# An attention and feed-forward kernel: attention's rows go through HBM, the stream is normalised on ScalarE, idle products stand in the fill, and every engine's order is new

## What is computed

```python
def reference(x, ln_w, ln_b, w_q, w_kv, w_o, theta, weight, bias):
    x = x + layernorm(attention(layernorm(x), ...))
    x = x + layernorm(ffn(layernorm(x), weight, bias))
    return x

# attention: 16 heads of 16, h = layernorm(x) * ln_w + ln_b
q, k, v = rope(h @ w_q), rope(h @ w_k), h @ w_v
s = k @ q.T * 16**-0.5                # per head
t = 1 + s + 0.5 * s * s               # a second-order "softmax"
wv = (t / t.sum(-1)) @ v
out = wv @ w_o
# ffn: rows and weights are rounded to a 6-bit grid in blocks of 32, then multiplied
out = dequantised(x) @ dequantised(weight).T + bias
```

## Time and profile before

| | |
|---|---|
| median of three runs | 645.11 us (644.78 to 649.38) |
| the profiled execution | 651.11 us |
| its span, first to last instruction | 648.8 us |
| mean granted TensorE clock | 0.985 |
| busy: PE, DVE, ACT, POOL | 615.9, 594.8, 530.0, 449.3 us |

### The profile page before, as it was taken

How to read it: one execution, slowest core, us unless ns; L and a number is a source line. 1 busy time by engine, 2 the same in 40 slices (tenths; PEclk the granted TensorE clock), 3 DMA queues, 4 the chain that set the end, 5 groups by cost and what they waited for, 6 DMA issues and landing times. The chain is left out here.

```text
span 648.8 us, 20724 instructions
## 1 busy us (share of the span) xinstructions
PE 615.9 (95%) x6620; PEld 457.7 (71%) x6620; DVE 594.8 (92%) x1489; ACT 530.0 (82%) x1448; POOL 449.3 (69%) x785
## 2 busy tenths in 40 slices
PE   6889999999999999999999999999999999999974
PEld 5666667676776776777777777767777766788763
DVE  5799899899899989999999999989999999987796
ACT  4347788888788897989888888978888888999973
POOL 3475466677777878788777867767877777765464
PEclk9699999999999999999999999999999999999996
DMA  7101031222223232232323232223223212230201
GB/s 245 34 2 42 20 76 30 72 63 65 50 72 88 70 91 68 75 84 67 62 67 83 77 86 73 69 57 101 60 68 92 76 39 41 68 91 18 68 26 49
DMA packets 52362, 43.51 MB, mean 67 GB/s; under 512 B 7201, under 2 KB 48545, under 8 KB 52257
## 3 DMA queue, kind: packets, MB, share of 16 engines
q1 hardware_dynamic: 51440, 41.42, 24.1%
q10 hardware_dynamic: 816, 0.79, 0.4%
HBM read 18.65 MB, written 8.39 MB: 42 GB/s over the span
## 5 line engine op out<-in xcount | busy, mean ns | idle before, releaser
L1168 ACT ACTIVATE feat<-ps_f 128x512 f32<-128x512 f32 x256 | 144.4, 599 | 4.9 <-PE ps_f L852 4.3
L691 DVE TENSOR_TENSOR kf<-kf 128x896 f32<-128x896 f32 (+1 forms) x128 | 131.2, 1027 | 1.8
L852 PE MATMUL ps_f<-qT,selr 128*128 128x512 f32 x320 | 122.1, 435 | 1.8 <-ACT qT L1236 1.3
L691 POOL TENSOR_TENSOR kf<-kf 128x224 f32<-128x224 f32 x64 | 76.5, 1195 | 13.3 <-DVE kf L1515 11.1
L1015 PEld LDWEIGHTS ps_mt<-kf,vp 128*32 128x32 f32 x2048 | 64.1, 110 | 30.0 <-issue 28.3
L1015 PE MATMUL ps_mt<-kf,vp 128*32 128x153 f32 x2048 | 79.7, 296 | 0.6 <-DVE kf L691 0.6
L1725 POOL TENSOR_TENSOR qsp<-kf,qsp 128x256 fp32r<-128x256 f32 x64 | 58.6, 916 | 9.8 <-ACT qsp L1259 9.6
L852 PEld LDWEIGHTS ps_f<-qT,selr 128*128 128x128 f32 x320 | 52.8, 190 | 15.2 <-issue 11.0
L913 PE MATMUL ps_o<-feat,main 120*32 120x512 f32 x448 | 59.7, 604 | 0.0
L916 PE MATMUL ps_o<-feat,rm 128*32 128x512 f32 x448 | 58.6, 593 | 0.0
L788 PE MATMUL ps_qk<-wkqv_h,hT_l 128*128 128x512 f32 x128 | 52.4, 409 | 3.3 <-DVE wkqv_l L1425 3.3
(11 more groups left out here) (199 smaller groups left out, 1885.2 us busy)
## 6 DMA issues: line engine op xcount, KB each, us to landing
xc<-L_attn_x SPq DMA_DIRECT2D x16, 512.0 KB, 4.5
result<-fin SPq DMA_DIRECT2D x64, 128.0 KB, 2.0
xa<-L_attn_x SPq DMA_DIRECT2D x15, 512.0 KB, 4.1
heads_out<-osb SPq DMA_DIRECT2D x224, 32.0 KB, 2.0
shares<-sums SPq DMA_DIRECT2D x112, 64.0 KB
sums<-osb SPq DMA_DIRECT2D x224, 2.0 KB
wkqv<-L_attn_w_kv ACTq DMA_DIRECT2D x2, 256.0 KB, 4.9
xa<-L_attn_x SPq DMA_DIRECT2D x1, 384.0 KB, 6.2
```

The costliest lines, as they stand in the source:

```text
L691: return eng.tensor_tensor(dims(row, F_MAIN, [[FW, heads], [HD, NR - 1], [1, HD]]), dims(row, F_LIN, [[FW, heads], [0, NR - 1], [1, HD]]), ...
L852: pe.matmul(ps_f[i % 2][:, :], selr[:, i], queries, start=True, stop=True).then_inc(sel_done, 1)
L1168: act.activation(feat[:, p2, i], ps_f[i % 2][:, :], ACT.Square).then_inc(squared, 1)
```

## The change

1. `move_quad` issues one transfer per quad, all of a quad's osb, 256 KB, into a tensor in HBM (`rows`). New on SP, once per sequence: `fetch_heads` brings the denominators into `sums` (one transfer) and the results into `heads_out` (two of 256 KB, with a head's dimension outermost, so that a partition is dimension times heads plus head); `store_inverses` writes the reciprocals to HBM; `spread_shares` reads them back as two transfers of 256 KB for all four tiles. `normalise_attention` waits for both. `copy_quad` waits until osb's last content has been moved. The rows of w_o are loaded in the same new order, and the path of the last two sequences writes in it.
2. `normalise_x` moves from DVE to ACT, as Identity with a scale and a bias per partition. The bias, minus mean times rstd, is a new instruction on POOL, `shift_x`. `rstd_x` and `shift_x` wait until z of two tiles before is made.
3. `IDLE["fill"]` has 15 entries at PE's places 1 to 32: 30 products of 128 columns.
4. `constant` and `rest_terms` are split in two each (`sum_linear`, `scale_terms`); `weight_size` waits for `turn_ready`.
5. All places in `ORDER` are new. A sequence takes 58 places on PE, 75 on ACT, 81 on DVE, 52 on POOL and 13 on SP.

```diff
 ORDER = {
...
+IDLE = {"fill": (1, 1, 1, 4, 4, 6, 7, 10, 14, 19, 23, 24, 32, 32, 32,), "drain": ()}
...
-            sp.dma_start(wo[:], w_o.rearrange("(c p) n -> p c n", p=P)).then_inc(wo_in, 16)
+            for c in range(CH):
+                sp.dma_start(wo[:, c], w_o.rearrange("(h d) n -> d h n", d=HD)[:, c * HC:(c + 1) * HC]).then_inc(wo_in, 16)
...
             def move_quad(t):
-                par, quad, s = t.par, t.tile, t.seq
-                if quad == 0:
-                    wait(sp, norm_ready, NT * (s - 1))
-                    for tile in range(NT):
-                        wait(sp, shares_in[tile], 16 * CH * s)
+                par, quad = t.par, t.tile
+                wait(sp, heads_in[par], 16 * CH * (t.load - 1))
+                wait(sp, sums_in, 16 * (t.seq - 1))
                 sp.wait_ge(o_copied, t.n)
-                for part in range(NT):
-                    sp.dma_start(sums[part * H + HQ * quad:part * H + HQ * (quad + 1)],
-                                 osb[HD:P:VW, par, quad, part * P:(part + 1) * P]).then_inc(sums_in, 16)
-                for h in range(HQ):
-                    row = HD * (HQ * (quad % 2) + h)
-                    sp.dma_start(heads_out[row:row + HD, par, quad // 2], osb[VW * h:VW * h + HD, par, quad]).then_inc(heads_in[par], 16)
+                sp.dma_start(rows[par, quad], osb[:, par, quad]).then_inc(moved[par], 16)
+
+            def fetch_heads(t):
+                par, s = t.par, t.seq
+                wait(sp, inverses_out, 16 * s)
+                sp.wait_ge(moved[par], 16 * NQ * t.load)
+                by_row = rows[par].rearrange("q (h r) n -> r (q h) n", r=VW)
+                sp.dma_start(sums[:, :], by_row[HD]).then_inc(sums_in, 16)
+                wait(sp, norm_ready, NT * (s - 1))
+                for c in range(CH):
+                    sp.dma_start(heads_out[:, par, c], by_row[0:HD, c * HC:(c + 1) * HC]).then_inc(heads_in[par], 16)
+
+            def store_inverses(t):
+                s = t.seq
+                for c in range(CH):
+                    wait(sp, shares_in[c], 16 * s)
+                sp.wait_ge(inverted, s + 1)
+                sp.dma_start(inverses, sums[:, :]).then_inc(inverses_out, 16)
 
             def spread_shares(t):
                 s = t.seq
+                sp.wait_ge(inverses_out, 16 * (s + 1))
                 wait(sp, norm_ready, NT * s)
-                sp.wait_ge(inverted, s + 1)
-                for tile in range(NT):
-                    for c in range(CH):
-                        first = tile * H + c * HC
-                        sp.dma_start(shares[:, c, tile * P:(tile + 1) * P],
-                                     dims(sums[first:first + HC, 0:1], 0, [[0, HD], [1, P]])).then_inc(shares_in[tile], 16)
+                for c in range(CH):
+                    sp.dma_start(shares[:, c], dims(inverses, c * HC * T, [[T, HC], [1, T]], [0, HD])).then_inc(shares_in[c], 16)
...
+            def normalise_x(t):
+                act.wait_ge(x_centred, t.n)
+                wait(act, zT_done, t.n - 2)
+                act.activation(z[:, t.two, 0:D - 1], xa[:, t.par, t.tile, 0:D - 1], ACT.Identity,
+                               bias=centre_x[:, t.two:t.two + 1], scale=rs["x"][:, t.two:t.two + 1]).then_inc(z_ready, 1)
...
-            def normalise_x(t):
-                dve.wait_ge(rstd["x"], t.n)
-                wait(dve, zT_done, t.n - 2)
-                dve.tensor_scalar(z[:, t.two, 0:D - 1], xa[:, t.par, t.tile, 0:D - 1], mv[:, t.two, 0:1], rs["x"][:, t.two:t.two + 1],
-                                  ALU.subtract, ALU.mult).then_inc(z_ready, 1)
...
             def normalise_attention(t):
...
-                    dve.wait_ge(heads_in[t.par], 16 * H * t.load)
-                    dve.wait_ge(shares_in[t.tile], 16 * CH * (t.seq + 1))
+                    dve.wait_ge(heads_in[t.par], 16 * CH * t.load)
+                    for c in range(CH):
+                        dve.wait_ge(shares_in[c], 16 * (t.seq + 1))
...
             def rstd_x(t):
+                wait(pool, z_ready, t.n - 2)
                 inverse_root("x", t)
+
+            def shift_x(t):
+                pool.wait_ge(rstd["x"], t.n)
+                wait(pool, z_ready, t.n - 2)
+                pool.tensor_scalar(centre_x[:, t.two:t.two + 1], mv[:, t.two, 0:1], rs["x"][:, t.two:t.two + 1], -1.0,
+                                   ALU.mult, ALU.mult).then_inc(x_centred, 1)
```

More of the change, by code:

```diff
@@ L62 @@
[L62 to L67, removed]
@@ new lines @@
+        "high_v": ((12,), (), ()),
+        "normalise_x": ((2, 9, 10, 17, 18, 29, 32, 43, 63, 65, 81, 86, 106, 113, 124, 135, 178, 184, 214, 223, 251, 271,
+            296, 312, 328, 354, 372, 388, 404, 429, 444, 463, 479, 499, 517, 542, 546, 581, 592, 616, 627, 655, 676,
+            692, 706, 732, 749, 768, 778, 798, 822, 833, 864, 871, 888, 903, 924, 940, 959, 978, 1004, 1029, 1041,
+            1069,), (), ()),
+        "sines": ((6,), (), ()),
+        "split_ffn_weight": ((111,), (), ()),
@@ L349 @@
     "constant": "sequence", "copy_ffn_weight": "once", "copy_main": "sequence", "copy_rest": "sequence", "copy_sums":
-    "sequence", "ffn_weight_mean": "once", "fold_kq": "once", "fold_v": "once", "frequencies": "once", "high_kq":
-    "once", "high_v": "once", "invert_denominators": "tail", "invert_sums": "spread", "load_again": "load",
-    "load_stream": "load", "low_attention": "body", "low_attention_late": "tail", "low_ffn_weight": "once", "low_kq":
-    "once", "low_v": "once", "low_wo": "once", "move_quad": "body", "rest_matrix": "sequence", "rest_terms": "sequence",
@@ L359 @@
-    "weight_size": "once", "wo_mean": "once"}
-IDLE = {"fill": (), "drain": ()}
+    "sequence", "fetch_heads": "spread", "ffn_weight_mean": "once", "fold_kq": "once", "fold_v": "once", "frequencies":
+    "once", "high_kq": "once", "high_v": "once", "invert_denominators": "tail", "invert_sums": "spread", "load_again":
+    "load", "load_stream": "load", "low_attention": "body", "low_attention_late": "tail", "low_ffn_weight": "once",
+    "low_kq": "once", "low_v": "once", "low_wo": "once", "move_quad": "body", "rest_matrix": "sequence", "rest_terms":
@@ new lines @@
+    "sequence", "scale_ln": "once", "scale_terms": "sequence", "sines": "once", "split_ffn_weight": "once", "split_wo":
+    "once", "spread_shares": "spread", "store_inverses": "spread", "sum_bias": "once", "sum_linear": "sequence",
+    "sum_wo": "once", "tables": "once", "turn_attention": "tail", "turn_ffn_weight": "once", "turn_quads": "tail",
+    "turn_sums": "sequence", "turn_weights": "once", "warm_up": "once", "weight_cast_high": "once", "weight_cast_low":
+    "once", "weight_choice": "once", "weight_distance_sizes": "once", "weight_distances": "once", "weight_high": "once",
@@ L363, in places @@
+    "weight_low": "once", "weight_result": "once", "weight_scales": "once", "weight_size": "once", "wo_mean": "once"}
+IDLE = {"fill": (1, 1, 1, 4, 4, 6, 7, 10, 14, 19, 23, 24, 32, 32, 32,), "drain": ()}
 def places(table, count):
@@ L424, with dims @@
 NSMALL = P + 32 + 2 * HD + 1 + 2 * CH
-def dims(ap, offset, free):
-    return bass.AP(ap.tensor, ap.offset + offset, [list(ap.ap[0])] + [list(d) for d in free])
+def dims(ap, offset, free, first=None):
+    return bass.AP(ap.tensor, ap.offset + offset, [first or list(ap.ap[0])] + [list(d) for d in free])
 def sandwich(nc, x, w_q, w_kv, w_o, weight, bias, identity, columns, selection, out):
@@ L580, in sandwich @@
         sums = sb("sums", [HEADROWS, P])
+        rows = nc.dram_tensor("rows", [2, NQ, P, T], F32).ap()
+        inverses = nc.dram_tensor("inverses", [H * T // P, P], F32).ap()
         rden = sb("rden", [P, H])
@@ L737, in step @@
                 spread(n, "spread_shares", spread_shares)
+                spread(n, "store_inverses", store_inverses)
+                spread(n, "fetch_heads", fetch_heads)
                 body(n, "move_quad", move_quad)
@@ L1313, in step @@
                 setup(n, "centre_bias", centre_bias)
+                each(n, "normalise_x", normalise_x)
                 each(n, "high_h", high_h)
@@ L1520, in products, with sum_linear @@
                 k_products(dve, t, half * H // 2, H // 2 - half * HG).then_inc(feat_ready[half], 1)
+            def sum_linear(t):
+                dve.wait_ge(mt_copied, t.seq + 1)
+                wait(dve, cb_ready, t.seq)
+                dve.tensor_reduce(lins[:], mts[:, :, F_LIN:NF], AX.X, ALU.add).then_inc(lins_done, 1)
             def constant(t):
-                dve.wait_ge(mt_copied, t.seq + 1)
-                dve.tensor_reduce(lins[:], mts[:, :, F_LIN:NF], AX.X, ALU.add).then_inc(lins_done, 1)
                 dve.wait_ge(lins_done, t.seq + 1)
@@ L1530, in constant, with scale_terms @@
                                          ALU.mult, ALU.add).then_inc(cb_ready, 1)
-            def rest_terms(t):
+            def scale_terms(t):
                 dve.wait_ge(mt_copied, t.seq + 1)
@@ L1638, in step @@
             def step(n):
```

(4 more changed lines are left out.)

492 lines of the change are left out of this document (253 added, 239 removed), and 99 rows, old and new, of the table ORDER.

## The result

The changed kernel takes 659.47 us (median of four runs, 657.76 to 660.67), the kernel before 645.20 us on the same chip: a ratio of 1.0194, 95% interval 1.0164 to 1.0225 (the two medians alone give 1.022, inside it). It is slower by 1.9%, where 630 us were predicted. The profiled execution took 660.67 us, its span is 658.8.

What follows compares the result with a forecast made beforehand. The prediction took DVE as the tightest engine, PE close behind. Body -12, fill -4, shares +1 and the rest 0 summed to -15 us, from 645.1 to 630 us, range 614 to 649.

Steps and rivals of the forecast that it cites:

- DVE is the tightest engine, with PE close behind: Body before the change: DVE needs 35.9 us a sequence, PE about 35.2, against 36.6 in that stretch.
- the largest term: Body, sequences 5 to 15: moving normalise_x off DVE cuts 36.9 to 35.8 us a sequence, 12 us saved.
- PE's need: Body: 34.2 us a sequence from tiles without uneven gaps plus 1.0 for once-per-sequence matrices, about 35.2 us.
- The step from 35.2 to 35.8: Body: pitch set above PE's 35.2 us, nearer the lower end of today's 2% to 4% over the heaviest engine.
- The first rival: Body: PE is the bound already, pitch stays 36.9 us and only the fill gives, 641 us; chance 0.16.
- Part 1's prices: normalise_x: 0.465 us leaves DVE, 0.51 net (0.42 to 0.60) joins ACT each time; shift_x on POOL hidden.
- The fill's -4: Fill, 30 to 153 us: some 16 normalisations leave DVE, 4 us saved, ends 0 and 6.7.
- The sums: Part 2, chain behind the reciprocals: inverses, two issues and landing total 7.0 us (6.2 to 8.7), room 7.6.
- The price of +1: Part 2, DVE's waits for shares: 1 us more on the path, ends 0 and 15.
- The slower rival: Shares come late at DVE's normalise_attention; at 2 us a sequence 28 us are lost, 657 us; chance 0.12.
- Part 3: Idle products in PE's fill: taken as 0, from -4 if they keep the clock up to +5.4 if they delay work.
- The rival that ACT becomes the bound: Body: waiting on ACT makes 36.2 us a sequence, 8 us saved, 637 us; chance 0.12.

Runs made afterwards that it cites:

- before_less_dve: Kernel before, order untouched, with normalise_x on 32 of 255 columns and the first statistics on 64 of 256 on DVE; ratio 1.0008 to the kernel before.
- after_less_act: Changed kernel, order untouched, with normalise_x and the squares of the three later norms on 64 columns; ratio 1.0183 to the kernel before, changed kernel 1.0194.

## Why the prediction was wrong

**The bound: the step that failed.** "DVE is the tightest engine, with PE close behind" led to the largest term, 36.9 to 35.8 us a sequence, -12 us in the body. That term came out at nothing: by the cuts the pitch is 36.95 us before and 37.03 after, and relief of DVE alone didn't move the time (before_less_dve). PE's time counts most: of what was put in, 28 of some 38 us came through on PE, 13.4 of 30.7 on DVE, 4.3 of 38.4 on ACT. PE's need was put at 35.2 us by taking each gap over the best spacing of starts as slack; the run with more PE work has room for up to some 36.2 (38.52 less 2.4). The step from 35.2 to 35.8 slipped as well: 36.9 over 35.3 to 35.9 is 2.8% to 4.5%, not 2% to 4%, and over 35.2 that gives 36.2 to 36.8, a gain of 1 to 8 us, not 12. The first rival had the engine right, but not the time, 641. Why PE's starts aren't closer where they are uneven, the runs don't say.

**Part 1's prices** were near: ACT's instruction takes 602 ns, the upper end of the row estimate, against 465 on DVE, and its load alone costs 4.3 us in the old order. The Trainium skill (ScalarE: Activation LUTs, Rules for kernel authors) keeps adds and multiplies on VectorE; the two durations agree. The time goes either way: alone in the old order the move costs 2.4%, in the new order undoing it costs 1.2%.

**The fill's -4** is a loss of 2 by the cuts. PE idles 4.1 us from 15 to 30 and 3.6 from 30 to 80, about as much as before (3.2 and 4.2) and more than before with the idle products alone (2.7 and 2.1). The cause is open.

**Part 2.** The sums held, their terms less: 7.55 us behind the reciprocals in the last sequence, forecast 7.0 (6.2 to 8.7), in it a median 3.6 us for a read put at 2.8; 10.3 us of DVE's waits, forecast "not much over 10". The price of +1 didn't: the growth of the wait was counted, 1.2 us, but a wait's cost is not its length. 9.1 us of it cost 5.2 before, 10.3 cost 11.3 after, part of that in the drain, 96.2 us with the wait and 90.7 without, where the clock also fell behind it in the one trace and not in the other. The slower rival had the place right and the size wrong: seven sequences of 14 are late, not all. That its 657 us lie near 659.47 is luck: they net off 16 us of gains that didn't come. The Trainium skill (DMA: Bandwidth & Descriptors, Anatomy of one DMA) warns of a long receipt when a write goes to HBM; its section is on transfers that GpSimd issues, these are SP's. By the medians no such receipt is seen: 2.1 and 1.8 us for the writes, 2.0 inside SBUF. Single writes of the reciprocals took up to 3.7 us, single transfers inside SBUF up to 3.4.

**Part 3** at 0 was right within what can be measured: in the kernel before the clock from 15 to 30 us went from 0.66 to 1.00, and the time by 0.2%, with an interval that still touches 1. The 0.66 is an end of its range: in the 12 traces without the idle products this stretch has 0.66 to 0.89, in six of the eight with them 1.00, in the other two 0.77 and 0.89.

**A term that the sum put at nothing** is the new order, whose places were weighed for the reciprocals alone. With neither kernel waiting for shares the changed one is still 1.0% slower, give or take 0.3. ACT's load isn't the cause (after_less_act), and undoing parts 1 and 2 makes it slower still; whether it is the order, and what in it, stays open. The rival that ACT becomes the bound is out.

## What to carry to other kernels

To find out whose time counts among engines that are all over 80% busy, add a known time, counted by starts, to each at unchanged places: the one of which most comes through is nearest to the bound. Relief of the others was worth nothing here. Cost a new order as a change of its own, since parts 1 and 2 were each worth over 1% in the order made for them and cost 2.4% and 7% in the other. Weigh a wait by what stands behind it, above all where the work runs out: take it away in both kernels before calling its growth small.

## What the runs showed of the hardware that was not expected

PE was busy 4.26 of the 5.80 us to 579.8, at a clock of 1.00, and stood still from 578.3 to 580.5; from 579.8 on the granted clock was 0.51 for 7.0 us, though PE worked in 6.27 of them, and 1.00 again after that. A read of 256 KB from HBM took 3.6 to 3.7 us to land by the medians, nearer to the 4.5 us for 512 KB than the write's 2.1 us for the same size.
